# GpSimd's order in the third attention, a flag folded into a multiplication, the turning transfers issued in pairs, and another split of weights in the opening of a four-layer residual net

## What is computed

```python
x = x + _L0_cond_ref(...)   # attention, 16 heads of 32, with a coherence gate and a field
x = x + _L1_cond_ref(...)   # masked attention, rmsnorm, modulated by the conditioning
x = x + _L2_cond_ref(...)   # x + attention(norm(x)); then + swiglu(norm(x))
x = x + _L3_cond_ref(...)   # a filter along the sequence and two quaternion products
```

```python
attn = jax.nn.softmax(jnp.einsum('bhid,bhjd->bhij', q, k) / jnp.sqrt(jnp.float32(HD)), axis=-1)
coh = jax.nn.sigmoid(jnp.tanh(comb @ Wc1.T + bc1) @ Wc2.T + bc2).transpose(0, 2, 1)
mod = attn * coh[..., None]
mod = mod / (mod.sum(-1, keepdims=True) + 1e-08)
mod = (1.0 - fi) * mod + fi * fa[:, None, :, None]
```

```python
def _tc_rmsnorm(x, t, gw, gb, bw, bb):
    g = (t @ gw.T + gb)[:, None, :]
    b = (t @ bw.T + bb)[:, None, :]
    inv_rms = jax.lax.rsqrt(jnp.mean(x * x, axis=-1, keepdims=True) + EPS)
    return g * x * inv_rms + b
```

## Time and profile before

| | |
|---|---|
| median of 3 runs | 2946.81 us (2944.68 to 2946.95) |
| profiled execution | 2946.95 us, span 2945.2 us |
| TensorE (PE) busy | 2832.9 us, 96% of the span |
| TensorE's weight loads (PEld) | 2488.1 us, 84% |
| VectorE (DVE) | 2077.9 us, 71% |
| ScalarE (ACT) | 1386.7 us, 47% |
| GpSimd (POOL) | 672.8 us, 23% |

### The profile page before, as it was taken

How to read it: one execution, slowest core, us unless ns; L and a number is a source line. 1 busy time by engine, 2 the same in 40 slices (tenths; PEclk the granted TensorE clock), 3 DMA queues, 4 the chain that set the end, 5 groups by cost and what they waited for, 6 DMA issues and landing times. The chain is left out here.

```text
span 2945.2 us, 69390 instructions
## 1 busy us (share of the span) xinstructions
PE 2832.9 (96%) x26999; PEld 2488.1 (84%) x26999; DVE 2077.9 (71%) x3640; ACT 1386.7 (47%) x2254; POOL 672.8 (23%) x563
## 2 busy tenths in 40 slices
PE   6999999998999999988999998999999999999997
PEld 5899999998899999888888887788888888888886
...
GB/s 141 105 133 117 134 131 136 128 122 187 133 112 105 110 111 100 126 176 135 109 103 115 106 114 128 129 69 60 57 71 84 90 98 29 58 44 51 48 29 43
DMA packets 514586, 300.44 MB, mean 102 GB/s; under 512 B 411776, under 2 KB 484608, under 8 KB 513952
## 3 DMA queue, kind: packets, MB, share of 16 engines
...
## 5 line engine op out<-in xcount | busy, mean ns | idle before, releaser
L746 PE MATMUL att_bank_a<-keep_hh,keep_wgateh 128*128 128x256 f32 x1536 | 449.3, 293 | 0.9 <-ACT att_af L915 0.9
L964 ACT ACTIVATE att_shifted<-att_shifted,keep_lift 128x512 f32<-128x512 f32 x384 | 276.2, 719 | 341.2 <-DVE att_shifted L1133 341.2
L747 PE MATMUL att_bank_a<-keep_hh,keep_wgatel 128*128 128x256 f32 x1536 | 435.3, 283 | 0.0
L748 PE MATMUL att_bank_a<-keep_hl,keep_wgateh 128*128 128x256 f32 x1536 | 435.1, 283 | 0.0
L1730 DVE TENSOR_TENSOR mlp_act_t<-mlp_bank_u,mlp_sg 128x512 f32<-128x512 f32 x128 | 88.4, 690 | 453.5 <-ACT mlp_sg L1636 449.8
L1636 ACT ACTIVATE mlp_sg<-mlp_bank_g 128x512 f32<-128x512 f32 x128 | 76.7, 599 | 628.9 <-PE mlp_bank_u L1560 628.9
L1779 POOL TENSOR_TENSOR mlp_al<-mlp_act_t,mlp_ah 128x512 fp32r<-128x512 f32 x128 | 174.7, 1365 | 863.0 <-ACT mlp_ah L1642 863.0
L1137 DVE TENSOR_TENSOR att_pq<-att_shifted,att_pq 128x512 f16<-128x512 f32 x384 | 331.2, 865 | 45.2 <-ACT att_pq L959 42.6
L746 PEld LDWEIGHTS att_bank_a<-keep_hh,keep_wgateh 128*128 128x128 f32 x1536 | 294.6, 192 | 4.4 <-ACT att_af L915 1.1
L747 PEld LDWEIGHTS att_bank_a<-keep_hh,keep_wgatel 128*128 128x128 f32 x1536 | 295.1, 192 | 0.1
L748 PEld LDWEIGHTS att_bank_a<-keep_hl,keep_wgateh 128*128 128x128 f32 x1536 | 295.0, 192 | 0.0
...
## 6 DMA issues: line engine op xcount, KB each, us to landing
...
```

What stands on the lines that cost most here:

```text
L746: nc.tensor.matmul(out, w_h, x_h, start=first, stop=False)
L747: nc.tensor.matmul(out, w_l, x_h, start=False, stop=False)
L748: return nc.tensor.matmul(out, w_h, x_l, start=False, stop=last)
L964: nc.scalar.activation(shifted[:, u % 2], shifted[:, u % 2], ACT.Exp, bias=k["lift"][:, 0:1], scale=SCALE).then_inc(exp_done, 1)
```

## The change

The change has four parts.

- **GpSimd's list in layer three.** `norm_end` stood at the end of an iteration's list (for the iteration after the next), and so ahead of the first remainders of the following one. Now it stands between the first remainders and the third values of that following iteration.
- **The flag.** In layer two the product of the reciprocals with `any_key` is gone; the output multiplication takes the flag as its scalar (a `scalar_tensor_tensor`).
- **SyncE's list.** The two turns of a pair of units are issued one behind the other, and the piece's load, the swaps and the residual's transfers follow.
- **The conditioning and the opening.** `prepare` splits v's weights and x (ScalarE the high part, GpSimd the low part of x) with one staging tile; the attention loads and splits c, k, q and o by halves, at places given by `SPLIT_AT`, and begins with v's projections, then c's, k's and q's.

```diff
@@ -151,7 +151,8 @@
         ps = [ctx.enter_context(nc.psum_tensor(f"prep_ps{n}", [P, 512], F32)) for n in range(8)]
-        ws = Splitter(nc, hold, "prep", weights, [sb(f"stage{n}", [P, CH * E]) for n in range(2)])
+        ws = Splitter(nc, hold, "prep", weights, [sb("stage", [P, CH * E])])
+        x_loaded, x_high = sem("x_loaded"), sem("x_high")
         small_loaded, e2_loaded, late_loaded, ahead_loaded = sem("small_loaded"), sem("e2_loaded"), sem("late_loaded"), sem("ahead_loaded")
@@ -173,15 +174,20 @@
                 ws.load(sp, n)
-            for dst, src in ahead:
+            x, x_dram = ahead[0]
+            sp.dma_start(x, x_dram).then_inc(x_loaded, 16)
+            for dst, src in ahead[1:]:
                 sp.dma_start(dst, src).then_inc(ahead_loaded, 16)
-            sp.wait_ge(ahead_loaded, 16 * len(ahead))
+            sp.wait_ge(ahead_loaded, 16 * (len(ahead) - 1))
...
                 nc.gpsimd.memset(t[:], 1.0 if t is k["v1"] else 0.0)
+            high, low = x_split
+            pool.wait_ge(x_high, 1)
+            nc.gpsimd.tensor_tensor(low, ahead[0][0], f32(high), ALU.subtract)
@@ -240,6 +246,8 @@
                 ws.high(act, n)
+            act.wait_ge(x_loaded, 16)
+            nc.scalar.activation(x_split[0], ahead[0][0], ACT.Copy).then_inc(x_high, 1)
@@ -403,9 +411,9 @@
         halves = [slice(0, CH // 2), slice(CH // 2, CH)]
-        FIRST = 6
+        SPLIT_AT = {0: (0, 1), 7: (2, 3), 8: (4, 5), 10: (6, 7)}
         loads = [(a["L0_" + n][:, m * CH // 2 * E:(m + 1) * CH // 2 * E], flat3(wh[n][:, part]), flat3(wl[n][:, part]))
-                 for n in "cvo" for m, part in enumerate(halves)]
+                 for n in "ckqo" for m, part in enumerate(halves)]
         ws = Splitter(nc, hold, "att", loads, [spare[0][:], spare[1][:], vr[:].rearrange("p b e -> p (b e)")], staged=2)
@@ -482,8 +490,8 @@
             keys, values = [("k", 0), ("q", 0)], [("v", 0), ("v", 1)]
-            ahead = values + keys if values_first(i) else keys + values
-            return [("k", 1), ("q", 1), ("o", 0), ("o", 1)] + ([("c", 0), ("c", 1)] if lay(i + 1) == 0 else []) + ahead
+            hidden = [("c", 0), ("c", 1)] if lay(i + 1) == 0 else []
+            return [("k", 1), ("q", 1), ("o", 0), ("o", 1)] + (values + hidden + keys if values_first(i) else hidden + keys + values)
@@ -596,7 +604,7 @@
-            return 2 * (4 * i + j) if lay(i) < 2 else 4 * i + j + 4 * 2 * G
+            return 2 * (4 * i + j) if lay(i) == 0 else 4 * i + j + 4 * G
@@ -660,7 +668,9 @@
             sp.sem_inc(x_loaded, 16)
-            for n in range(ws.staged, FIRST):
+            sp.sem_inc(x_high, 1)
+            sp.sem_inc(x_split, 1)
+            for n in range(ws.staged, len(loads)):
                 if n == 4:
@@ -712,18 +722,20 @@
             def body(i):
-                for u in range(UNITS):
+                for u in range(0, UNITS, 2):
                     turn_probs(i, u)
+                    turn_probs(i, u + 1)
                     if u == 0 and piece_of(i) is not None:
...
                     swap(i, u)
-                    if u == 1 and post(i):
+                    swap(i, u + 1)
+                    if u == 0 and post(i):
                         load_residual(i - 1)
...
                         store(i - 1)
-                    if u == 5 and has(i, 2) and lay(i + 2) < 2:
+                    if u == 4 and has(i, 2) and lay(i + 2) < 2:
                         load(i + 2)
-                    if u == 7 and has_x(i, 3) and lay(i + 3) == 2:
+                    if u == 6 and has_x(i, 3) and lay(i + 3) == 2:
                         load(i + 3)
@@ -753,14 +765,14 @@
                         pe.wait_ge(a_free[bk], n)
-                    if isinstance(p, int) and p == 0 and m == 0 and kind in "cv":
-                        pe.wait_ge(ws.low_done, 2 * "cv".index(kind) + 2)
+                    if isinstance(p, int) and p == 0 and m == 0 and kind in "ckq":
+                        pe.wait_ge(ws.low_done, 2 * "ckq".index(kind) + 2)
                     if isinstance(p, int) and p > 0 and p % G == 0:
...
                         pe.wait_ge(new_weights["o", m], 32 * lay(p))
-                    if fill == (("c", 0) if lay(p) == 0 else ("v", 0) if values_first(body_of(p, fill)) else ("k", 0)):
+                    if fill == (("v", 0) if values_first(body_of(p, fill)) else ("c", 0) if lay(p) == 0 else ("k", 0)):
                         pe.wait_ge(x_split, p + 1)
@@ -891,7 +903,7 @@
                 if isinstance(i, int) and i == 0:
-                    pe.wait_ge(ws.low_done, FIRST)
+                    pe.wait_ge(ws.low_done, len(loads))
@@ -1019,11 +1031,9 @@
             act.wait_ge(eps_set, 1)
-            high_x(0)
             for s, pieces in enumerate(pieces_of(-1)):
-                if s < FIRST and s % 2 == 0:
-                    for n in (s, s + 1):
-                        ws.high(act, n)
+                for n in SPLIT_AT.get(s, ()):
+                    ws.high(act, n)
                 for fill, part in pieces:
@@ -1147,16 +1157,17 @@
                     nc.vector.tensor_tensor(r, r, cf[:].rearrange("p (b h) -> p b h", b=NB)[:, :, 4 * j:4 * j + 4], ALU.mult).then_inc(rz_step, 1)
-                if lay(i) == 1:
-                    nc.vector.tensor_scalar(r, r, k["any_key"][:, 0:1], None, ALU.mult).then_inc(rz_step, 1)
-                if lay(i) != 2:
                     dve.wait_ge(rz_step, z_turn(i, j) + 2)
...
                 scale = r.unsqueeze(3).broadcast_to([P, NB, 4, HD])
-                nc.vector.tensor_tensor(dst, src[:, :, :, 0:HD], scale, ALU.mult).then_inc(o_free, 1)
+                if lay(i) == 1:
+                    nc.vector.scalar_tensor_tensor(out=dst, in0=src[:, :, :, 0:HD], scalar=k["any_key"][:, 0:1], in1=scale,
+                                                   op0=ALU.mult, op1=ALU.mult).then_inc(o_free, 1)
+                else:
+                    nc.vector.tensor_tensor(dst, src[:, :, :, 0:HD], scale, ALU.mult).then_inc(o_free, 1)
@@ -1222,12 +1233,10 @@
             nc.vector.memset(eps[:], 1e-6).then_inc(eps_set, 1)
-            low_x(0)
             nc.vector.tensor_copy(tb[:], k["tanh_bias"][:, :, 0:NB]).then_inc(tb_ready, 1)
             for s, pieces in enumerate(pieces_of(-1)):
-                if s < FIRST and s % 2 == 0:
-                    for n in (s, s + 1):
-                        ws.low(dve, n)
+                for n in SPLIT_AT.get(s, ()):
+                    ws.low(dve, n)
                 for fill, part in pieces:
@@ -1369,6 +1378,8 @@
                     rest_of_values(i, b)
+                if positive(i) and pre(i - 1):
+                    norm_end(i + 1)
                 for b in range(NB):
@@ -1377,10 +1388,9 @@
                     low_t(i + 1)
-                if pre(i):
-                    norm_end(i + 2)
             iterate(pool, body)
+            norm_end(ALL + 1)
             low_x(ALL + 1)
@@ -1836,10 +1846,10 @@
             xin, spare = shared("xin", [P, CH, T], F32), [shared(f"spare{n}", [P, CH // 2 * E], F32) for n in range(2)]
-            early = [(a["L0_" + n], flat3(wh[n]), flat3(wl[n])) for n in "kq"]
+            early = [(a["L0_v"], flat3(wh["v"]), flat3(wl["v"]))]
             ahead = [(xin[:], a["x"][0])] + [(t[:], a["L0_c"][:, m * CH // 2 * E:(m + 1) * CH // 2 * E]) for m, t in enumerate(spare)]
             att_stored = nc.alloc_semaphore("att_stored")
-            phase(prepare, a, early, ahead)
+            phase(prepare, a, early, ahead, (hh[:, :, 0:T], hl[:, :, 0:T]))
             phase(attention, [a["x"], scratch[0], scratch[1]], scratch[0:3], wh, wl, a, *split, hh, hl, xin, spare, att_stored)
```

4 lines of the change are left out of this document (2 added, 2 removed).

## The result

The changed kernel takes 2912.39 us (median of 4 runs, 2911.36 to 2913.68) against 2945.74 us of the kernel before (median of 4, 2943.87 to 2946.95): 33.35 us less, a ratio of 0.9886 with a 95% interval from 0.9874 to 0.9898. The forecast was 2911.5 us, with a range from 2901 to 2928.

The account below looks back on a forecast made before the run. TensorE, busy for 96% of the span, was taken as the bound, so only its waits could be won. From 2946.95 us, -12 - 9 - 4 - 10.5 = -35.5 gave 2911.5 us, range 2901 to 2928.

Parts of the forecast that it names:

- A: Layer three, GpSimd's order: `norm_end` behind `att_vr` frees VectorE's low part L1137, ending TensorE's 1.1 us wait per iteration; -12 us.
- The reason: Layer three: `att_vr` back to back held VectorE's low part for 2.85 us; small TENSOR_SCALARs of `norm_end` would hardly hinder it.
- Rival 1: Layer three: back-to-back GpSimd instructions never let VectorE in, so L1137 waits for all eight; 2925.5 us, chance 0.17.
- the row of L1211 beside `norm_end`: Profile row: eight two-operand VectorE instructions take 2.30 us beside `norm_end` and 3.95 beside `att_vr`.
- B: Layer two, flag in the output multiplication: TensorE's waits for `att_of` go, iterations 28 to 30 shorten; -9 us.
- C: Weight swaps, SyncE's order: paired turns leave earlier, so TensorE waits less for turned tiles; -4 us, between 0 and -7.
- a quarter of the 8.4: Around iteration 15: of 8.4 us in four TensorE waits for turned tiles, 2 us were to go.
- the same share at the other swap (iteration 31): Second weight swap, iteration 31: SyncE's order was to gain the same share there as around iteration 15.
- D: Opening, only v split beforehand: first projection earlier (-5.7), wait for ScalarE's tanh gone (-3.1), low clock gone (-1.7); -10.5 us.
- 2: Opening: TensorE waits for k's and q's low weights, so the opening is won by half; 2917 us, chance 0.08.
- 3: Transitions, iteration 31 and neighbours: bytes moved set the time, so gains there shrink; 2920 us, chance 0.08.
- Rival 4: Layer three: `att_vr` starts before VectorE's scaling of x and delays the next projection; slower, 2956.5 us, chance 0.03.

## Why the prediction was right

**The sum.** Predicted -35.5 from 2946.95, measured -33.35 between medians. That the forecast of 2911.5 lies only 0.9 us off the 2912.39 is in part luck, since the kernel before measured 2945.74 this time. Taken alone and by the ratios, each of the four parts came within 2 us of its term; the intervals are wider than that, so this shows the sizes only roughly.

**A, -12 predicted, -10.3 measured alone.** L1147 was to take 0.7 to 1.1 us; it takes 0.69, and 0.80 to 0.91 in four iterations. The steady iterations were to lose 1.1 us; they lose 1.08 (33.50 to 32.42). The prediction counted thirteen of them, 34 to 46, for 14 us; 45 and 46 gain little, and the thirteen together give 11.8 (11.0 with this part alone). Two us were to come back in the transition; it was 2.8 with this part alone. Its reading that `att_vr` could start at 1443.96 took the end of both of ScalarE's copies; it starts right behind the first of the two, and nothing hangs on the half us.

The reason was right, and the rule beside it is right for one kind of instruction and wrong for the other: the Trainium skill ("SBUF — State Buffer", section "Who interferes with whom") has the later instruction blocked for the whole of the one that runs, which would let VectorE in after at most one. For `norm_end` the trace agrees: L1147 at 1389.97 ended 0.5 us behind the one multiplication beside it, and in the steady iterations one multiplication waits for L1147 (1.00 us for 0.45), though by the recorded starts it is 0.06 us ahead of it. For the first remainders it disagrees: cut into quarters, they held VectorE for 5.86 us, over eight and two further instructions. Rival 1's premise, that a series holds VectorE, is thus true of `att_vr`, and its conclusion false, since `norm_end` is not such a series. That the forecast came out rested on the row of L1211 beside `norm_end`: nothing in the prediction told why one series holds VectorE and the other does not, and the runs do not tell it either.

**B, -9 predicted, -7.4 alone, -8 within the whole.** The steady part was to be 3.4 us and is 2.2 (0.22 in each of ten iterations, where I had counted 0.3 in eleven). Of the 5.7 us in iterations 28 to 30 there are 3.9 with the flag alone, 2.0 of it in 28; the rest of the gain lay in 31, in 17 and in stretches of clock, which I had not counted. The wait of the weight loads for `att_of` between 880 and 1140 us is gone, as the sign said. The third operand costs 0.06 us, within its bounds.

**C, -4 predicted, -4.1 alone, -7 within the whole (the intervals just overlap).** Right in size and wrong in place, and this is the step that failed: "a quarter of the 8.4" was to come off in iteration 15, from the sixth turn, and "the same share at the other swap (iteration 31)". Iteration 15 keeps its long wait, 5.2 us, and takes 47.4 us for 46.7; iteration 31 shows nothing (44.9 with SyncE's order and 43.6 without it). The gain is in 16, 40.3 to 36.2, where short waits go and with them a stretch at the lower clock. The prediction named neither, so that its 4 us came out was luck.

**D, -10.5 predicted, -11.5 alone (10.9 by the starts of iteration 0).** The start of the first projection was to be 37.0 and is 36.43, VectorE was to be held for 1.1 us and is for 0.85. The wait of 3.14 us and the stretch at 0.50 behind it went, as said. The sign "no stretch of granted clock 0.50 in the first 60 us" did not come true: there still is one behind TensorE's rest from 30.6 on. Not counted was that it would be shorter, from 36.43 to 40.3 where it was from 42.73 to 48.

**The rivals.** 2 and 3 did not occur as priced, but 3's ground is partly true: what happens in iterations 29 to 33 does not follow from VectorE's instructions alone. Rival 4 did not occur: x's scaling, L1212 at 1450.05, takes 1.21 us, and `att_vr` begins at 1451.28, when it has ended. What decides is who starts first: L1212 does, by 1.2 us, the margin that the prediction named.
